# Layer-norm statistics of two sequences in one interleaved instruction, and a new order of work on every engine

## The reference

```
x = x + wkv(layernorm(x), ctx)        # decay scan along the 128 tokens, first mixer
x = x + down(silu(gate(n)) * up(n))   # n = layernorm(x); 256 -> 704 -> 256
# layernorm: (x - mean) / sqrt(var + 1e-5) over the 256 channels, no weights
# wkv: numerator and denominator are decayed running sums of exp(k)*v and exp(k), k = layernorm(x)
```

## Time and profile before

| | |
|---|---|
| median of 3 runs | 104.21 us (104.07 to 104.45) |
| profiled execution, first to last instruction (span) | 102.7 us |
| what lies around the span (median less span) | 1.5 us |
| busy: PE / DVE / ACT / POOL | 91.5 / 80.0 / 78.2 / 66.8 us |
| granted TensorE clock, mean over the span | 1.000 |
| input transfers | all but the outputs are over by about 27 us |

### The profile page before, as it was taken

The page is one execution under the profiler, slowest core; times in us unless marked ns, Lnnn a source line. Parts: engine busy times, 40 slices in busy tenths (PEclk is TensorE's granted clock), DMA queues, the critical chain, the costliest instruction groups (busy, mean ns, idle before and its releaser), DMA issues.

```text
span 102.7 us, 1698 instructions
## 1 busy us (share of the span) xinstructions
PE 91.5 (89%) x504; PEld 75.1 (73%) x504; DVE 80.0 (78%) x169; ACT 78.2 (76%) x136; POOL 66.8 (65%) x96
## 2 busy tenths in 40 slices
PE   3958976998799999996999999999999999999930
PEld 3957965996596778875788887887888778888610
DVE  1789899969998999799999998999863806543450
ACT  4371999989997879999999999999959634655300
POOL 2016465998799999894399779827899701764500
PEclk9999999999999999999999999999999999999999
DMA  1999999999000000000005000000500000400005
GB/s 32 307 379 405 403 321 388 343 387 343 34 0 0 0 0 10 0 0 0 0 0 203 1 6 0 0 3 0 203 1 0 0 6 3 183 21 0 0 28 189
DMA packets 6475, 10.78 MB, mean 105 GB/s; under 512 B 576, under 2 KB 3648, under 8 KB 6336
## 3 DMA queue, kind: packets, MB, share of 16 engines
q1 hardware_dynamic: 6320, 10.62, 28.9%
q10 hardware_dynamic: 144, 0.03, 0.2%
HBM read 8.55 MB, written 2.10 MB: 104 GB/s over the span
## 4 chain that ended last, share of the span: by engine, by line
PE 27%; POOL 17%; ACT 15%; issue 14%; DMA 11%; DVE 6%; SPq 4%; POOLq 2%; DVEq 1%; ACTq 0%
PE ps_f L728 16%; DMA xc<-x_ch 11%; POOL hl L346 11%; PE ps_d L745 4%; ACT ek L405 4%; PE ps_f L756 3%; ACT L374 2%; POOL xc L311 2%; ACT nt L434 2%; SPq L228 2%; PE ps_x L698 2%; ACT xh L445 2%; DVE h L631 1%; POOL rs L323 1%; POOLq L59 1%
## 5 line engine op out<-in xcount | busy, mean ns | idle before, releaser
L728 PE MATMUL ps_f<-xh,wgu_r 128*128 128x512 f32 (+1 forms) x94 | 36.3, 391 | 0.6 <-DVE xl L616 0.4
L728 PE MATMUL ps_f<-xl,wgu_r 128*128 128x512 f32 (+1 forms) x94 | 35.1, 378 | 0.0
L346 POOL TENSOR_TENSOR hl<-h,hh 128x512 fp32r<-128x512 f32 x20 | 25.6, 1293 | 9.3 <-ACT hh L476 9.2
L631 DVE SCALAR_TENSOR_TENSOR h<-ps_f,vec,sil 128x512 f32<-128x512 f32 x20 | 14.9, 744 | 9.2 <-PE ps_f L728 6.2
L728 PEld LDWEIGHTS ps_f<-xh,wgu_r 128*128 128x128 f32 x94 | 17.7, 188 | 5.5 <-issue 1.4
L728 PEld LDWEIGHTS ps_f<-xl,wgu_r 128*128 128x128 f32 x94 | 17.7, 188 | 2.8
L756 PE MATMUL ps_f<-ident 128*128 128x128 f32 x110 | 15.5, 296 | 1.9 <-POOL ident L266 1.6
L465 ACT ACTIVATE sil<-ps_f,vec 128x512 f32<-128x512 f32 x20 | 13.7, 688 | 4.0 <-PE ps_f L728 3.8
L745 PE MATMUL ps_d<-hh,wd_r 128*128 128x512 f32 x40 | 16.3, 407 | 0.1
L756 PEld LDWEIGHTS ps_f<-ident 128*128 128x128 f32 x110 | 14.5, 211 | 2.1 <-POOL ident L266 1.6
L476 ACT ACTIVATE hh<-h 128x512 fp32r<-128x512 f32 x20 | 12.5, 629 | 4.6 <-DVE h L631 4.5
(11 more groups left out here) (73 smaller groups left out, 133.8 us busy)
## 6 DMA issues: line engine op xcount, KB each, us to landing
xt<-x_tok SPq DMA_DIRECT2D x8, 256.0 KB, 7.3
xc<-x_ch SPq DMA_DIRECT2D x4, 512.0 KB, 9.6
out_ch<-xc SPq DMA_DIRECT2D x8, 256.0 KB, 2.5
wgu<-w_gu SPq DMA_DIRECT2D x1, 1408.0 KB, 8.6
vc<-v_ch SPq DMA_DIRECT2D x2, 512.0 KB, 9.4
wd<-w_d SPq DMA_DIRECT2D x1, 768.0 KB, 10.0
vt<-v_tok SPq DMA_DIRECT2D x2, 256.0 KB, 5.3
vt<-v_tok SPq DMA_DIRECT2D x1, 512.0 KB, 12.3
```

Of the source, the lines that this page charges most:

```text
L346: nc.gpsimd.tensor_tensor(hl[:, m, :], h[:, n % HS, :], hh[:, m, :].bitcast(F32), ALU.subtract).then_inc(s_hl, 1)
L631: nc.vector.scalar_tensor_tensor(h[:, n % HS, :] if m < FULL else up, up, vec[r, V_US + m:V_US + m + 1], sil[r, n % 2, :], ALU.mult, ALU.m ...
L728: last = nc.tensor.matmul(ps_f[:, i % RING, ts], w, a, start=c == 0 and x is xh, stop=c == CC - 1 and x is xl)
```

## The change

Three things change together.

1. **Statistics.** `st1` and `st2` become three numbers per sequence. One `bn_stats` per unit reads both sequences alternately (b0 c0, b1 c0, b0 c1, b1 c1, ...): 512 elements with a hop of 256 elements (1 KiB) at every step. The even positions are then all of one sequence and the odd ones all of the other, so the two triples are already complete: no `bn_aggr`. The readers take `st[..., 1]` as mean and scale `st[..., 2]` by 1/256 inside instructions that existed already. 32 stats and 32 aggregates become 16 stats of twice the length.
2. **Order.** The call lists of POOL, ACT, DVE and PE are new throughout.
3. **Transfers.** The residual load of group 0 goes ahead of the down weights, x of unit 4 ahead of v of units 2 and 3, v of the last group ahead of the last two residual loads, and x of unit 7 goes last.

Unused alternatives (`HIGH_POOL`, `FIN_ACT`, `RSTD_POOL`, all empty) are removed; they issued nothing.

```diff
-        st1 = sb("st1", [P, B, 6])
-        mv1 = sb("mv1", [P, B, 2])
+        st1 = sb("st1", [P, B, 3])
...
-            load_x(0); load_x(1); load_x(2); load_x(3); load_v(0); load_v(1)
-            sp.dma_start(wgu[:, :, :, :].rearrange("p c m n -> p (c m n)"), w_gu).then_inc(s_wgu, 16)
-            sp.dma_start(wd[:, :, :].rearrange("p m n -> p (m n)"), w_d).then_inc(s_wd, 16)
-            load_res(0); load_v(2); load_x(4); load_x(5); load_v(3); load_res(1)
-            load_x(6); load_x(7); load_v(4); load_res(2); load_res(3)
+            load_x(0); load_x(1); load_x(2); load_x(3); load_v(0); load_v(1); load_wgu(); load_res(0); load_wd()
+            load_x(4); load_v(2); load_x(5); load_x(6); load_v(3); load_res(1); load_v(4); load_res(2); load_res(3)
+            load_x(7)
...
-                nc.scalar.activation(lv1[:, q], mv1[:, q, 1], ACT.Ln, bias=epsc[:, 0:1]).then_inc(s_lv1, 1)
+                nc.scalar.activation(lv1[:, q], st1[:, q, 2], ACT.Ln, scale=1.0 / C, bias=epsc[:, 0:1]).then_inc(s_lv1, 1)
...
-                for b in range(u * UB, (u + 1) * UB):
-                    last = nc.vector.bn_stats(st1[:, b, :], xt[:, b, :])
-                last.then_inc(s_st1, 1)
-
-            def aggr1(u):
-                dve.wait_ge(s_st1, u + 1)
-                for b in range(u * UB, (u + 1) * UB):
-                    last = nc.vector.bn_aggr(mv1[:, b, :], st1[:, b, :])
-                last.then_inc(s_mv1, 1)
+                nc.vector.bn_stats(st1[:, seqs(u), :].rearrange("p b k -> p (b k)"),
+                                   xt[:, seqs(u), :].rearrange("p b c -> p c b")).then_inc(s_st1, 1)
...
+                nc.vector.bn_stats(st2[:, seqs(u), :].rearrange("p b k -> p (b k)"),
+                                   x1_bank(u).rearrange("p (b c) -> p c b", b=UB)).then_inc(s_st2, 1)
...
-            rstd1(0); expk(0); elift_(); rstd1(1); expk(1); rstd1(3); log_den(0); expk(2); recip(0); wcheck(0)
+            rstd1(0); elift_(); expk(0); rstd1(1); rstd1(3); expk(1); expk(2); log_den(0); expk(3); recip(0)
...
-                warm(2); n_T(0); warm(1); n_T(1); e_T(4); p_T(3); gatea(0); upa(0); gatea(1); x1_T(2); gate(0); gate(1); up(0); up(1)
+                p_T(3); gatea(0); upa(0); gatea(1); e_T(4); gate(0); x1_T(2); up(0); gate(1); up(1); gate(2); up(2)
```

More of the change, by code:

```diff
@@ L499, in _ @@
-            high_h(18); silu(20); high_h(19); silu(21); high_h(20); high_h(21); silu(22); silu(23); high_h(22)
-            high_h(23)
+            rstd1(0); elift_(); expk(0); rstd1(1); rstd1(3); expk(1); expk(2); log_den(0); expk(3); recip(0)
+            wcheck(0); log_den(1); recip(1); wcheck(1); wcheck(2); log_den(2); rstd2a(0); recip(2); rstd2a(1)
+            rstd1(5); norm2(0); norm2(1); log_den(3); high_n(0); expk(4); recip(3); high_n(1); expk(5); tables(SILU)
+            silu(0); silu(1); high_h(0); silu(2); norm2(2); high_h(1); silu(3); high_h(2); high_n(2); high_h(3)
@@ new lines, in _ @@
+            silu(4); silu(5); tables(LN_EXP); log_den(4); rstd1(7); recip(4); norm2(3); expk(6); high_n(3); high_h(4)
+            high_h(5); log_den(5); expk(7); recip(5); tables(SILU); silu(6); norm2(4); silu(7); high_n(4); high_h(6)
+            high_h(7); silu(8); silu(9); tables(LN_EXP); log_den(6); high_h(8); recip(6); norm2(5); tables(SILU)
+            silu(10); high_n(5); high_h(9); silu(11); high_h(10); high_h(11); silu(12); tables(LN_EXP); log_den(7)
+            norm2(6); recip(7); tables(SILU); silu(13); high_n(6); high_h(12); silu(14); silu(15); high_h(13)
@@ L667, in _ @@
-            numer(7); gated(13); finish(1); low_n(6); gated(14); stats2(7); aggr2(7); gated(15); gated(16); gated(17)
-            low_n(7); low_rest(17); gated(18); gated(19); finish(2); gated(20); gated(21); gated(22); gated(23)
-            low_rest(23); finish_c(0); finish_c(1)
+            stats1(0); stats1(1); lift_(); decay_(); stats1(2); stats1(3); scan_e(0); denom(0); scan_p(0); scan_e(1)
+            numer(0); denom(1); scan_p(1); numer(1); scan_e(2); denom(2); stats2(0); stats1(4); stats1(5); stats2(1)
@@ L671, in _ @@
+            mulp(7); low_rest(11); denom(7); gated(12); scan_p(7); numer(7); gated(13); low_n(6); gated(14); finish(1)
+            stats2(7); gated(15); gated(16); gated(17); low_n(7); low_rest(17); gated(18); gated(19); finish(2)
+            gated(20); gated(21); gated(22); gated(23); low_rest(23); finish_c(0); finish_c(1)
         @block.tensor
@@ L797, in _ @@
+            e_T(3); x1_T(1); count(); warm(1); p_T(2); warm(8); n_T(0); n_T(1)
             pe.wait_ge(s_wgu, 16)
```

156 lines of the change are left out of this document (48 added, 108 removed).

## The result

The changed kernel takes 105.84 us, the median of 4 runs (104.87 to 106.5); the kernel before, beside it, 104.14 us (103.82 to 104.45). The ratio is 1.0134, with a 95% interval of 1.0091 to 1.0176: slower by 1.3%, where 102.1 us and "faster" were forecast. The span of the profiled execution is 103.7 us against 102.7.

What follows compares the result with a forecast made beforehand. The bound was the FFN stream: its start, set by ACT, plus PE's matmuls and holes. Start -1.6 and stream -0.5 gave -2.1 us: span 100.6, plus 1.5 around it, 102.1 us; own range 101.3 to 103.0, overall 101.0 to 104.0.

Steps and rivals of the forecast that it cites:

- Statistics: On DVE: each new 512-element stats instruction takes 0.68 us, relieving DVE of 4.8 us.
- (a): DVE statistics: interleaved read costs more than a contiguous one; 103.3 us at 1.0 per instruction, 104.2 at 1.2; chance 0.12.
- (b): DVE statistics: they become DVE's bound, from about 1.25 us per instruction; 106.7 us at 1.5; chance 0.05.
- Rival (d): PE's clock at half for the first 4 us of the FFN stream: 2 us go, 104.1 us; chance 0.03.
- The start: Up to the fourth product: ACT's earlier expk(1) brings it to 30.1 instead of 31.71, a gain of 1.6 us.
- what could end later on the way: Start: check of delays before high_n(0) at 24.3; all judged free, tightest 0.3 us at stats2(1).
- the rival on PE's clock: Same as Rival (d): counts 60 idle-filling matmuls in place of 55; half clock would give 104.1 us; chance 0.03.
- the walk: Start, step by step through the engines' lists: high_n(0) about 24.3, silu(0) 29.2 to 29.4, fourth product 30.1.
- The stream: PE's FFN matmuls after the fourth product: same number, so only holes can go; net -0.5 us.
- The end: After the last matmul pair: last residual and output, 4.4 us, claimed not changed.
- Rival (c): Start gained and lost again through slips where an instruction precedes a late one: 103.6 to 104.1 us; chance 0.10.
- two places: In the start: stats2(1) on DVE with 0.3 us to spare, and PE's branch, costing about 0.9, with nothing to spare.

Runs made afterwards that it cites:

- c_before: The kernel before, unedited, run again as a control with its own trace: 104.05 us, ratio 0.9994.
- c_after: The kernel after (the full change), unedited, run again for a second trace: 105.52 us, ratio 1.0117.
- e_after_near: Kernel after, with PE ending its list only when a product shortly before the last one (in down(21)) is done: 104.52 us, ratio 1.0035.
- e_warm12: Kernel after without the 11 added idle-filling matmuls ahead of e_T(0): 103.82 us, ratio 0.9977.
- e_w12_near: e_best_near without its two unused tiles, so with the addresses of the kernel after: 102.47 us, ratio 0.9834.
- e_best_near: Kernel after without the 11 filling matmuls, with two unused 320 B tiles (old addresses), PE's list held until a product in down(21): 101.96 us, ratio 0.9798.
- e_best_near2: Same source as e_best_near, run again: 102.03 us, ratio 0.9802; its profiled execution took 103.41 us.
- e_pad_tail: Kernel after, 11 filling matmuls kept, with two unused 320 B tiles and PE's list held until its last product: 104.14 us, ratio 1.0002.
- e_w12_tail: Kernel after without the 11 filling matmuls, with PE's list held until its last product is done: 103.36 us, ratio 0.9863.

## Why the prediction was wrong, step by step

The time splits into three stages, read from PE in order of time: the start of the fourth product, from there to the start of the last matmul (252 matmuls of 128x512 in every trace), and from there to the span's end. All in us.

| trace | fourth product | to the last matmul | to the end |
|---|---|---|---|
| before | 31.71 | 66.38 | 4.61 |
| c_before | 31.25 | 66.38 | 4.60 |
| forecast | 30.1 | 65.9 | 4.6 |
| after | 30.86 | 66.26 | 6.57 |
| c_after | 31.68 | 66.25 | 5.82 |
| e_after_near | 31.90 | 66.27 | 4.62 |
| e_warm12 | 29.73 | 66.26 | 6.31 |
| e_w12_near | 29.83 | 66.27 | 4.61 |
| e_best_near | 29.79 | 65.76 | 4.62 |
| e_best_near2 | 31.27 | 65.74 | 4.60 |

So the span of 103.7 instead of the forecast 100.6 is 0.8 us of start, 0.4 of stream and 2.0 of end.

**Statistics: right.** 0.68 us forecast, 0.69 to 0.70 measured, in PSUM too; DVE fell to 76.7 us (about 75 forecast). Rivals (a) and (b) are out. The Trainium skill, "Vector Engine (DVE) Microarchitecture Reference", section "Measured stream behaviour on trn2": its sentence on one stream that alternates between two regions at the full rate agrees with the 0.69 to 0.70 us here; its 1.73 ns per hop, by which an estimate of the instruction was 1.03 us, does not apply. Rival (d) is out too: the granted clock was 1.00 from 28 to 98 us in the kernel after.

**The start: failed, -1.6 us forecast, -0.85 in the profiled execution and nothing in three other traces.** The failed step is the list of "what could end later on the way". It priced PE only at the branch; the 11 matmuls added ahead of `e_T(0)` were counted under the rival on PE's clock and given no time. They put `e_T(0)` at 8.22, 1.3 us behind a ready `ek(0)`, `scan_e(0)` at 8.93, 0.61 us after DVE was free for it, `high_n(0)` at 25.06 (24.3 forecast), `silu(0)` at 30.02 (29.3), the fourth product at 30.86 (30.1). ACT's own part was nearly right: `expk(1)` at 8.80 (8.45 forecast), `expk(2)` behind a wait of 0.34 (0.35). Without the 11 matmuls the walk holds within 0.3 us. e_best_near, ACT's `high_n(0)` and `silu(0)`, then PE's fourth product:

```profile
24.00 0.60 ACT L406 ACTIVATE xh<-ps_x 128x512 fp32r<-128x512 f32 x1
28.95 0.69 ACT L426 ACTIVATE sil<-ps_f,vec 128x512 f32<-128x512 f32 x1
```
```profile
29.79 0.47 PE L664 MATMUL ps_f<-xh,wgu_r 128*128 128x512 f32 x1
```

The fourth product is 1.9 us earlier than in the earlier trace rows. Two rows of before could have warned (PE in order of time):

```profile
7.12 0.66 PE L679 MATMUL ps_a<-ident,ek 128*128 128x128 f32 x4 [1.07 <-ACT ek L405]
7.61 1.28 PE L756 MATMUL ps_f<-ident 128*128 128x128 f32 x10
```

`ek(0)` had kept PE waiting 1.07 us. Filling takes at least 0.11 to 0.13 us a record (10 in 1.28 us), and 22 records more, 2.4 us even at that pace, were to stand in front of it. The kernel before has the same fault at another place, on its own critical chain: POOL ended `add_y(1)` at 20.6, but 24 filling records held `x1_T(1)` until 21.22, and DVE waited for it.

```profile
18.54 2.84 PE L756 MATMUL ps_f<-ident 128*128 128x128 f32 x24
```
```profile
21.86 0.76 DVE L600 BATCH_NORM_STATS2 st<-ps_d 128x6 f32<-128x256 f32 x2 [0.81 <-PE ps_d L698]
```

**The stream: holes right, the pace wrong.** -0.5 us was forecast; with the old addresses it is -0.6 (66.38 to 65.76), in the kernel after -0.1. `up(14)` came at 70.24 behind a wait for `silu(13)`, as described, 1.0 us late, of which 0.8 is the start's delay. But "the matmuls are the same in number, so only holes can go" failed: each became 3.3 ns longer, 0.8 us over 252, of which 0.5 shows in the stage.

**The end: "is not changed" failed, the largest term in the profiled execution.** It grew by 2.0 us there, and holding PE's list at the right place gives back 1.0 us in the kernel after (105.52 to 104.52, the same chip in two groups; ratios 1.0117 and 1.0035) and 1.4% without `warm(11)` (e_warm12 0.9977, e_w12_near 0.9834, two chips). This cause was no rival of mine.

**Rival (c) was half right.** Of its two places the branch was not late, but `stats2(1)` was: it ended at 21.62, where 20.5 was forecast, and ACT stood still for it. That was the filling matmuls' delay arriving there; e_best_near has no such wait, and e_best_near2 has one of 1.71 us, from the late x of unit 5. The margin of 0.3 us that the prediction gave this place is as thin as it said.

```profile
21.66 0.30 ACT L382 ACTIVATE ve<-st,epsc 128x2 f32<-128x2 f32 x1 [0.56 <-DVE st L541]
```

**What lies around the span: 1.8 us, not 1.5.** The prediction took a median less the span of one execution; in the 19 traces since, the time of the profiled execution itself less its span is 1.8 to 1.9.

**The sum as it came out.** Along one path: 105.52 us; `warm(11)` away -1.70 (103.82); end held -1.35 (102.47, another chip); old addresses -0.44 (102.03). That this meets the forecast's 102.1 is in part luck: it is another kernel than the one forecast, its span is 0.4 us shorter (100.2 against 100.6), and 0.3 more lies around it. The steps aren't independent: `warm(11)` cost 1.29 in one pair, 1.70 in another, and e_after_near's twelve runs spread from 103.6 to 104.9. One reason may be what shows in the traces: the filling matmuls start 213 ns apart at first and 112 ns later, and the number of slow steps varies from one execution to the next (13 in the kernel after, 22 to 24 in c_after, e_pad_tail and e_after_near). With all 46 records in front of `e_T(0)` it starts at 8.2 or at 9.1 to 9.3. The profile's granted clock (the 1.00 ahead of the transfers' share) does not explain the slow steps, kernel after:

```profile
1.00:5.00 4.00, 3.43 (x18) 3.43 (x19) 1.66 (x5) 2.12 (x6) 0.29 (x1) 1.00 0.72 223
```

What ends them stays open, and so does why an address shift of 640 B slows a matmul.

## What to carry to other kernels

Walk every engine's list when an order changes, idle filling included: what fills a wait must end before the wait does, at the slowest pace that the trace shows for it. When a tile's size changes, compare the matmul step before crediting or blaming the edit; two unused tiles gave 0.5 us back here. And the end of an engine's list is an event: look where its instruction fetches fall beside the last transfer. e_best_near, with the three mended, runs at 0.980 of the kernel before. Work out every stage of a profile apart (start, stream, end): a stage that agrees to 0.1 us over six traces settles what medians with a spread of 1 us leave open.

## What the runs showed of the hardware

- A `bn_stats` that alternates between two regions 1 KiB apart takes 0.69 to 0.70 us for 512 elements, as PSUM and SBUF source alike.
- The step of a 128x512 matmul was 229 to 230 ns with the moving operands at the places of the kernel before or 256 B above them per partition, and 233.1 to 233.3 with them 384 or 640 B below, in all 20 traces (distances by the declared sizes).
- PE's branch at the end of the `If` has a record of 3.3 to 3.9 us. It began as DVE ended the result that the last product waits for. Two 16 KB instruction fetches followed, 0.9 to 1.6 us each. One DMA engine's share of the last output landed 1.0 us or more late beside one; and in five of the six traces in which PE's list ended after its last product, SP's issue of the last output beside one took 1.0 to 1.3 us instead of 0.33 (in the sixth, e_w12_tail, the fetch began only as the issue ended, and packets came late instead).
